# Second layer of a two-layer graph network on one core: products of two blocks in one step, roots and factors two blocks at a time, one row in 22 on GpSimd

## What is computed

```python
edge_index = jnp.stack([src, dst])
h = jnp.maximum(_layernorm(x, axis=-1), 0.0)
x = x + _L0_gnn_ref(h, edge_index, L0_gnn_W_self, L0_gnn_b_self, L0_gnn_W_neigh, L0_gnn_b_neigh)
h = jnp.maximum(_layernorm(x, axis=-1), 0.0)
x = x + _L1_gnn_ref(h, edge_index)
...
norm = deg_inv_sqrt[src] * deg_inv_sqrt[dst]
msgs = x[src] * norm[:, None]
out = jax.ops.segment_sum(msgs, dst, num_segments=n)
return jax.nn.relu(out)
```

## Time and profile before

| | us |
|---|---|
| median of 3 runs | 1458.72 (1457.88 to 1458.84) |
| the profiled execution's own time | 1462.61 |
| its span, first to last instruction | 1460.8 |
| layer one, most of it | 100 to 800 of the span |
| layer two, from its first products | 862 to 1461 |

### The profile page before, as it was taken

How to read it: one execution, slowest core, us unless ns; L and a number is a source line. 1 busy time by engine, 2 the same in 40 slices (tenths; PEclk the granted TensorE clock), 3 DMA queues, 4 the chain that set the end, 5 groups by cost and what they waited for, 6 DMA issues and landing times.

```text
span 1460.8 us, 30232 instructions
## 1 busy us (share of the span) xinstructions
PE 998.6 (68%) x9310; PEld 909.6 (62%) x9408; DVE 1047.7 (72%) x3040; ACT 1092.4 (75%) x2871; POOL 845.8 (58%) x1143
## 2 busy tenths in 40 slices
PE   2187888888888888888888804635457546644577
PEld 2177777777777777777778804535346435643566
DVE  7488777877777778787777537557577557755876
ACT  2388887888888888888888637658687669766967
POOL 4666666666666666666664075454664466456641
PEclk6599999999999999999999955555555555555555
DMA  5235555555555556555663256657686668666965
GB/s 178 96 92 183 159 173 168 169 176 170 165 176 167 173 175 181 163 170 161 182 180 126 107 168 178 179 174 221 183 259 204 181 185 262 197 181 189 266 193 192
DMA packets 82231, 259.39 MB, mean 178 GB/s; under 512 B 19986, under 2 KB 20356, under 8 KB 82116
## 3 DMA queue, kind: packets, MB, share of 16 engines
q1 hardware_dynamic: 58948, 210.86, 45.3%
q0 software_dynamic: 22400, 46.91, 13.5%
q10 hardware_dynamic: 768, 0.20, 0.1%
HBM read 152.93 MB, written 104.37 MB: 176 GB/s over the span
## 4 chain that ended last, share of the span: by engine, by line
ACT 37%; another core or an unknown queue 21%; DVE 18%; PE 11%; issue 11%; DMA 1%; ACTq 1%; DVEq 0%
ACT work L740 23%; DVE ST L1339 9%; ACT area L750 6%; PE p_O L970 5%; ACT area L755 4%; DVE area L1423 3%; ACT p_O L740 1%; DVE work L1356 1%; PE p_O L912 1%; PE p_T L970 1%; PE p_O L924 1%; PE p_T L862 1%; ACT sd L718 1%; PE p_T L887 1%
## 5 line engine op out<-in xcount | busy, mean ns | idle before, releaser
L740 ACT ACTIVATE work<-X,shift,scale 128x128 f32<-128x128 f32 x1372 | 559.7, 491 | 2.0 <-issue 1.0
L635 POOL DMA_INDIRECT X<-in_x,IDX x392 | 394.1, 1005 | 135.2 <-issue 102.8
L1339 DVE BATCH_NORM_STATS2 ST<-X 128x6 f32<-128x256 f32 x1176 | 406.4, 416 | 2.0
L970 PE MATMUL p_O<-work 32*128 32x128 f32 x1984 | 277.7, 436 | 121.4 <-remote 70.5
L635 POOL DMA_INDIRECT X<-x_table,IDX x294 | 289.3, 984 | 92.2 <-issue 79.4
L970 PEld LDWEIGHTS p_O<-work 32*128 32x128 f32 x1984 | 242.8, 323 | 149.7 <-remote 73.5
L1382 DVE TENSOR_TENSOR p_O<-p_O,rc 128x512 f32<-128x512 f32 x196 | 136.5, 696 | 157.9 <-PE p_O L912 138.8
L924 PE MATMUL p_O<-wsT,area 128*128 128x128 f32 x1568 | 215.2, 277 | 10.6 <-issue 4.7
L924 PEld LDWEIGHTS p_O<-wsT,area 128*128 128x128 f32 x1568 | 209.8, 192 | 18.0 <-issue 9.4
L912 PE MATMUL p_O<-wnT,area 128*128 128x128 f32 x1568 | 217.0, 282 | 1.4 <-issue 1.4
L740 ACT ACTIVATE p_O<-X,shift,scale 128x128 f32<-128x128 f32 x496 | 199.5, 444 | 17.4 <-DVE area L1423 13.9
(11 more groups left out here) (172 smaller groups left out, 1260.6 us busy)
## 6 DMA issues: line engine op xcount, KB each, us to landing
x_table<-area SPq DMA_DIRECT2D x98, 528.0 KB
X<-x_table SPq DMA_DIRECT2D x98, 528.0 KB
X<-in_x SPq DMA_DIRECT2D x98, 512.0 KB
out_x<-area SPq DMA_DIRECT2D x98, 512.0 KB
X<-in_x,IDX POOLq DMA_INDIRECT x392
X<-x_table,IDX POOLq DMA_INDIRECT x294
moved<-held SPq DMA_DIRECT2D x32, 12.2 KB
es<-in_src SPq DMA_DIRECT2D x1, 488.5 KB, 3.4
```

The costliest lines, as they stand in the source:

```text
L635: nc.gpsimd.indirect_dma_start(got(s)[:, k, 0:w], None, table, bass.IndirectOffsetOnAxis(ap=IDX[:, s, k:k + 1], axis=0)).then_inc(gathered ...
L740: last = nc.scalar.activation(o, row(l, s, r), ACT.Relu, bias=shift[:, s, r:r + 1], scale=scale[:, s, r:r + 1])
L970: last = nc.tensor.matmul(outs1[p][g][:, P * col:P * col + P], SEL[1][q, p, part_of, :], H[1][q, p, draw, :], start=False, stop=(half == 1 ...
L1339: last = V.bn_stats(ST[:, s, r:r + 2, :].rearrange("p r k -> p (r k)"), pair.rearrange("p r c -> p c r"))
```

## The change

It touches layer two alone.

- PE: step `off` issues the first half of block `off` and the second half of block `off-1` as one run of 16 products, in turn between them, on four row groups and four banks. It waits for `s_half` of the step before ahead of all 16. `agg_ready` of a block thus comes with the step of the next block.
- DVE and ACT: root, inverse, scale and shift are made for two blocks by one instruction each, in even steps (`together` gives 2 there, 1 for the very first two blocks, else 0). ACT issues the root after the sixth row (`MID1` = 6) of block `off+1`. DVE issues the inverse after the first half of `finish1`, then `select`, then scale and shift, then the second half of `finish1`.
- POOL: factors for two blocks at once, in even steps; before the gathers of an even step it makes the last row of block `off+1` (an odd block) with two `TENSOR_SCALAR` (`last_row1`). ACT leaves that row out, so odd blocks have 10 activations. PE waits for `row_ready` in odd blocks.

The diff, cut to its core:

```diff
+    def together(turn, off):
+
+        if not there(1, turn, off):
+            return 0
+        return 1 if first(place(1, turn, off)[0], 2) else 2 * (off % 2 == 0)
...
+    def lots(turn, off):
+
+        return 1 if first(place(1, turn, off)[0], 1) else turn * (RING[1] // 2) + off // 2 + 2
...
+            def last_row1(turn, off):
+
+                i, s, _ = place(1, turn, off)
+                r = ROWS1 - 1
+                pool.wait_ge(norm_ready[1], lots(turn, off))
+                pool.sem_inc(idx_seen[1], 1)
+                if not first(i, HR[1]):
+                    pool.wait_ge(agg_ready, i - HR[1] + 1)
+                    pool.sem_inc(idx_seen[1], 1)
+                h = H[1][:, off % HR[1], DRAWS - 1, :]
+                nc.gpsimd.tensor_scalar(h, row(1, s, r), scale[:, s, r:r + 1], shift[:, s, r:r + 1],
+                                        ALU.mult, ALU.add).then_inc(row_scaled, 1)
+                pool.wait_ge(row_scaled, pool_rows(turn, off))
+                pool.sem_inc(idx_seen[1], 1)
+                nc.gpsimd.tensor_scalar(h, h, 0.0, None, ALU.max).then_inc(row_ready, 1)
 
             def last_row(turn, off):
...
+            def factors(turn, off, n):
+
+                i, s, _ = place(1, turn, off)
+                for k in range(n):
+                    _, q, uses = place(1, turn, off + k)
+                    pool.wait_ge(x_loaded[q], (uses + len(range(q, NB, RING[0]))) * 16)
+                    pool.sem_inc(idx_seen[1], 1)
+                    pool.wait_ge(gathered[q], landed(1, q, turn, off + k))
+                    pool.sem_inc(idx_seen[1], 1)
                 if not first(i, RING[1]):
-                    pool.wait_ge(scale_made, i - RING[1] + 1)
+                    pool.wait_ge(scale_made, lots(turn, off) - RING[1] // 2)
                     pool.sem_inc(idx_seen[1], 1)
-                nc.gpsimd.tensor_tensor(factor[:, s, 0:BT], own(1, s)[:, :, D], own(1, s)[:, :, D], ALU.mult)
-                nc.gpsimd.tensor_tensor(factor[:, s, BT:ROWS1], got(s)[:, 0:DRAWS, D], moved[:, 2, 0:DRAWS, bass.ds(i, 1)
-                                                                                           ].rearrange("p k b -> p (k b)"),
-                                        ALU.mult).then_inc(factored, 1)
+                of_own = X[:, s:s + n, 0:BT * XW].rearrange("p n (j d) -> p n j d", j=BT)[:, :, :, D]
+                of_got = X[:, s:s + n, BT * XW:ROWS * XW].rearrange("p n (k d) -> p n k d", k=PAIRS)[:, :, 0:DRAWS, D]
+                nc.gpsimd.tensor_tensor(factor[:, s:s + n, 0:BT], of_own, of_own, ALU.mult)
+                nc.gpsimd.tensor_tensor(factor[:, s:s + n, BT:ROWS1], of_got,
+                                        moved[:, 2, 0:DRAWS, bass.ds(i, n)].rearrange("p k b -> p b k"), ALU.mult
+                                        ).then_inc(factored, 1)
...
+                if l == 1 and together(turn, off + 2):
                     if first(place(1, turn, off + 2)[0], 1):
                         pool.wait_ge(s_tab1, 2)
                         pool.sem_inc(idx_seen[1], 1)
-                    factors(turn, off + 2)
+                    factors(turn, off + 2, together(turn, off + 2))
+                if l == 1 and there(l, turn, off + 1) and by_pool(off + 1):
+                    last_row1(turn, off + 1)
                 gathers(l, turn, off + GATHER_AHEAD)
...
             def step1(turn, off):
-                if there(1, turn, off + 2):
-                    root(1, turn, off + 2)
                 if there(1, turn, off + 1):
-                    normalise(1, turn, off + 1, range(0, ROWS1))
+                    normalise(1, turn, off + 1, range(0, MID1))
+                if together(turn, off + 2):
+                    roots1(turn, off + 2, together(turn, off + 2))
+                if there(1, turn, off + 1):
+                    normalise(1, turn, off + 1, range(MID1, ROWS1 - by_pool(off + 1)))
...
+                this, last = there(1, turn, off), there(1, turn, off - 1)
+                if this:
+                    if by_pool(off):
+                        pe.wait_ge(row_ready, pool_rows(turn, off))
+                    pe.wait_ge(h_ready[1], 2 * i + 2)
+                    pe.wait_ge(sel_ready[1], i + 1)
+
+                if last:
+                    pe.wait_ge(s_half, i)
+                ends = [None, None]
+                for draw, part_of, col in ((0, 0, 0), (1, 1, 2), (2, 2, 0), (2, 3, 2)):
+                    for half in range(2):
+                        p = (off - half) % HR[1]
+                        if not (this, last)[half]:
+                            continue
                         for g in range(2):
                             q = slice(HALF * (2 * half + g), HALF * (2 * half + g) + HALF)
-                            last = nc.tensor.matmul(outs1[p][g][:, P * col:P * col + P], SEL[1][q, p, part_of, :],
-                                                    H[1][q, p, draw, :], start=False,
-                                                    stop=(half == 1 and part_of == 3), skip_group_check=True)
-                last.then_inc(agg_ready, 1)
+                            c = slice(P * (col + half), P * (col + half) + P)
+                            ends[half] = nc.tensor.matmul(outs1[p][g][:, c], SEL[1][q, p, part_of, :], H[1][q, p, draw, :],
+                                                          start=False, stop=(half == 1 and part_of == 3),
+                                                          skip_group_check=True)
+                if this:
+                    ends[0].then_inc(s_half, 1)
+                if last:
+                    ends[1].then_inc(agg_ready, 1)
...
             def step1(turn, off):
                 if there(1, turn, off + 3):
                     stats(1, turn, off + 3)
-                if there(1, turn, off + 2):
-                    inverse(1, turn, off + 2)
+                n = together(turn, off + 2)
                 if there(1, turn, off - 2):
                     finish1(turn, off - 2, 0)
-                if there(1, turn, off + 2):
-                    scales1(turn, off + 2)
-                if there(1, turn, off + SHIFT_AHEAD):
-                    shifts(1, turn, off + SHIFT_AHEAD)
+                if n:
+                    inverses1(turn, off + 2, n)
                 if there(1, turn, off + 1):
                     select(1, turn, off + 1)
+                if n:
+                    scales1(turn, off + 2, n)
+                    shifts1(turn, off + 2, n)
                 if there(1, turn, off - 2):
                     finish1(turn, off - 2, 1)
```

More of the change, by code:

```diff
@@ L617, in step @@
                     last_row(turn, off + 1)
-                if l == 1 and there(l, turn, off + 2):
+                if l == 1 and together(turn, off + 2):
                     if first(place(1, turn, off + 2)[0], 1):
@@ L725, in normalise @@
                 if rows[0] == 0:
-                    act.wait_ge(norm_ready[l], i + 1)
+                    act.wait_ge(norm_ready[l], lots(turn, off) if l else i + 1)
                     if not first(i, HR[l]):
@@ L766, in step0 @@
                     for i in due(off, ROOT_AHEAD):
-                        root(0, turn, i)
+                        root0(turn, i)
                 if there(0, turn, off):
```

88 lines of the change are left out of this document (45 added, 43 removed).

## The result

The changed kernel takes 1393.74 us (1392.26 to 1395.05, 4 runs), the kernel before beside it 1458.78 us (1457.88 to 1459.06): a ratio of 0.9555, 95% interval 0.9538 to 0.9571. The forecast was 1454.2 us with a range down to 1439. The direction was right, the size was not: 65 us instead of 4.5. The profiled execution took 1394.59 us, its span is 1392.8 us.

The account below looks back on a forecast made before the run. It took layer two as bound by ACT in five blocks of eight and by PE's 22.5 us pause otherwise. Ten turns saved 4.0 us, the last 12 blocks 0.5: 1458.7 - 4.5 = 1454.2 us, range 1439 to 1473.

Parts of the forecast that it names:

- What bounds the kernel: Layer two: ACT sets five blocks in eight at 4.43 us each, PE's 22.5 us pause the rest of a 49.1 us turn.
- part 4: PE's pause in layer two: expected at the same place of the code, again with five blocks between release and next pause.
- Parts 1 and 2: ACT in layer two: less work, 8.28 instead of 8.86 us a pair, but a new wait on DVE makes it 8.78.
- Part 3: PE's run of 16 products in layer two: 2.1 us, bounds 2.1 and 4.2, with nothing gained on the path.
- Part 5: A layer-two turn of eight blocks: 0.4 us less, so 4.0 in ten turns and 0.5 in the last 12 blocks.
- Part 6: POOL in layer two: 9.25 us a pair against ACT's 8.78, costed at nothing thanks to cover of 4 us or more.
- Part 7: POOL's last-row operations may meet DVE's comparison at a shared port in layer two: 0 to 0.54 us a pair.
- B: Rival, chance 0.10: a sixth block in each layer-two turn, 4.0 us a turn, 40 in all, 1498 us.
- C: Rival, chance 0.17: POOL's last row gets in the way, by port or POOL's own pace; pair 9.32 us, total 1470.
- A: Rival, chance 0.16: ACT's whole saving is had, a pair takes 8.28 us, total about 1441 us.
- E: Rival, chance 0.05: ACT's idle is 0.6 us instead of 0.5, so the gain is gone: 1458 us.
- D: Rival, chance 0.10: the pauses fall otherwise, one more or less at 15.2 us on the chain: 1439 or 1470 us.

Follow-up runs that it names:

- Run 3: PE's 98 layer-two blocks written out instead of a hardware loop: kernel before 1428.29 us against 1426.63, changed kernel 1369.59 us (ratio 0.9596).
- run 5: Changed kernel from layer two's ninth block on: one gather a block instead of three, 1289.85 us; three gathers of 4 numbers instead of 132, 1370.15 us.
- run 1: Kernel before with only PE's new order of products: 1388.83 us against 1426.63 (ratio 0.9727), later 1400.45 against 1430.24 (0.9778).
- run 6: Unread POOL instruction before each block's gathers: kernel before 1239.32 us, changed with all rows on ACT 1202.56; changed with factors moved 1228.23; before 1184.48.

## Why the prediction was wrong

*What bounds the kernel, and part 4.* This is the step that failed: "I take the pause as a given of PE's instruction stream" and "I expect it at the same place of the code". That PE awaits only its own signal was right, and so was the place where the pause lands on ACT. But the signal is sent in time and comes late. Run 3 excludes the instruction stream, run 5 names POOL's gathers. The pause was the largest entry of the chain with an unnamed releaser, and I read on without asking what every other engine did during it. POOL's rows across it would have shown one unbroken burst. In nine of the ten pauses the time from the start of the first stand to the end of the second is 22.3 to 22.9 us, however it is split (9.4 and 10.0 us once, 22.3 in one piece another time; the odd one out has stands of 12.6 and 18.8). That was in the trace as well, and a constant is a hint at a process with a length of its own. What stands in its place: no pause of 22.5 us per turn but 6.5 us in each of four pairs, of which DVE's 2.4 us reach the path, so that eight blocks take 4 x 10.85 = 43.4 us where 48.6 were forecast.

*Parts 1 and 2, ACT and the new chain.* Right: ACT's even block starts 0.45 us late after the scale, shift and `finish1`, where 0.50 was forecast. It did not matter, as the odd block waits 2.03 us for DVE, which waits for the late `agg_ready`.

*Part 3, PE.* Right: 16 products in one run take 2.09 us, 2.1 forecast. "Nothing is gained on the path" was wrong where signals are late: run 1 gives 30 to 38 us for the order alone. A block needs one late signal less in a row, since `s_half` and `agg_ready` travel together with one burst; that reading is argued and not shown.

*Part 5.* A turn with 0.4 us less was the forecast; it has 49.0 - 43.4 = 5.6 less. Ten such turns are 56 of the 65 us.

*Part 6, POOL at nothing.* This step failed too. Its pair was sized well (9.25 forecast, 9.40 seen), its cover was not. "It's slower than the pace but only between pauses" tied POOL's slack to a pause that POOL itself makes. Where there is no pause, 9.40 against 8.86 is the bound, and PE waits for POOL's row, which the prediction named as the sign that the cover was wrong. The change then costs 27 us.

*Part 7, the port.* It happens: `L619` lasts 0.93 us beside the comparison (1210.95) and 0.54 otherwise (1057.30). The rule that the prediction cites from the Trainium skill, "SBUF — State Buffer", section "SBUF: two separate sides" (such a pair excludes each other for the whole instruction), agrees with both rows. It moved nothing, as POOL waits 1.2 us in each pair there.

*The rivals.* B had the right mechanism in its words ("If the signal of the run before the pause is held to the end of the second stand") and the observation for it, that DVE saw nothing until 1200.86. It was dismissed since PE's own signal came at 1193.6. Both were late, and only asking when the signals arrive, not which, would have told it. C is what happens where nothing is late (+2.35%, where +0.8% was given), by its second mechanism, POOL's own pace; its first, the port, has no part there (`L619` lasts 0.54). A (no idle on ACT ahead of even blocks) and E (0.6 us of it) did not come, as 0.45 was seen; D expected one pause more or less, and all ten went.

## What to carry to other kernels

When the largest entry of the chain has no named releaser, look at what every engine does in that time and when it ends, POOL first, before calling it fixed. An engine that is "ahead" may be setting the time through what it does to others: here, breaking up POOL's gathers by the row was worth 49 us, more than the new order on PE (30 to 38) or the work saved on ACT and DVE. And a gain that rests on a wait nobody can explain should be measured on several occasions, since it was -4.5% on one and +2.35% on another.

## What the runs showed of the hardware

- While POOL issues indirect DMAs back to back (every 1.25 to 1.3 us), semaphore signals carried by PE's products can be seen up to 22.3 us late. Signals of ACT and DVE are not held in this way: of those recorded after 880 us in the changed kernel, 168 of ACT and 291 of DVE, none is over 0.3 us behind the end of its instruction; in the kernel before eight of 609 are, by 2.8 us at most. In the pair shown, within POOL's burst of gathers, DVE's inverse starts 0.03 us after ACT's root ends (1214.84 and 1214.81), and ACT's block at 1212.18 starts 0.1 us after DVE's `finish1`. The width of the gathers has no part (4 numbers or 132: 1370.15 and 1369.94 us), their number has (one instead of three a block: 1289.85).
- Where PE's signals are late, many updates of the other engines have no record at all: in the changed kernel 66 of ACT's 234 and 135 of DVE's 426 are missing. With one gather a block 7 of 229 and 8 of 411 are, where nothing is late 3 of 169 and 2 of 304. Whether the recording of events has a share in the lateness, or only suffers with it, was not tested.
- The lateness is not always there. Of six comparisons after the first, the kernel before took 1427, 1427 and 1430 us in three, with late signals in layer two of every kernel run beside it but the one with fewer gathers, and 1184, 1185 and 1183 in three, with none. It is the same program; one chip number occurs in both groups. All three of the second group had a kernel with the added instruction of run 6 among them and none of the first had; whether that is chance can't be told from these runs. What sets the condition stays open.
- In the late condition layer one suffers as well: the first products of layer two end at 850 to 864 us, and at 744 to 749 us where nothing is late. Signals of PE are late there too (run 5).
- A gather's row ends after 0.95 us, and the signals come 1.5 to 2.1 us later than the last row's end. The Trainium skill, "Perfetto Trace Analysis", section "DMA Instruction — SWDGE (GPSIMD)", says that the profile's end of such an instruction is the moment when its descriptors have been written, not when the transfer is done. These rows are in keeping with that but don't show it, as they hold nothing of descriptors. Why PE's signals should wait for it, no run says.
